# Two token pairs per turn in a 128-expert loop, expert counts formed on the matrix engine, and a shared final combination

## The chip, the cores and the metric

The kernel runs on one core of one Trainium2 chip. The metric is the device time of one launch in microseconds; three runs of the kernel before gave 1128.76, 1126.37 and 1127.86, so the median is 1127.86. In the text PE is TensorE, DVE is VectorE, ACT is ScalarE, POOL is GpSimd and SP is the engine that issues most transfers.

## The reference

Four sequences of 512 image tokens pass through softmax attention, get 77 text tokens appended (589 tokens, five tiles of 128 with the last partly empty), then a selective scan, a mixture of 14 experts, a causal attention, and last a mixture of 128 experts with two experts for each token. Layer normalization stands ahead of each of the last four. The change concerns the last two stages.

```python
scores = jnp.einsum('nqd,nkd->nqk', Q, K) / scale      # causal mask, softmax, times V
...
logits = xt @ wg                                       # 256 -> 128 experts
e1 = jnp.argmax(gates, -1); e2 = argmax of the rest
loc1 = (cumsum(mask1)[e1]) - 1                         # place of the token within its expert
loc2 = (cumsum(mask2)[e2] + counts1[e2]) - 1
buf  = rows placed at e*64 + loc (dropped from place 64 on)
yb   = jnp.einsum('ecd,edf->ecf', buf.reshape(128, 64, 256), we)
y    = (g1*v1) * yb[idx1] + (g2*v2) * yb[idx2]
h    = h + y
```

## The kernel before, in words

Every engine has one program, written out by hand in its order, and they meet only at semaphores. The token rows `Hs` are 20 tiles of 128 rows by 256 (`NB` = 4 sequences, `NT` = 5 tiles each).

**Causal stage.** For each sequence b, `project(b)` forms Q, K and V and `attend(b)` goes through five query tiles i: scores, mask and row maximum (`maxima`, DVE), exponential (ACT), transposes of the probabilities (L1267), their copy `PT4` (DVE, L2360), product with V (L1286), and the update of `Hs` (L2378). The routing of sequence b-1 to experts is woven in: normalized rows `xa5` (`rows5`), their turn (`turn_row`, L1160), copy `xaT5` (`turned5`, L1636), `logits` (L1166), `take_logits` (L2235) and `best_two`. For b of 2 and 3 the places of sequence b-2 are woven in too: `hots` makes the one-hot table `hot5` (L2253), `rank` on PE (L1181 to L1191) gives cumulative counts in three parts, `first_rows` on DVE (L2266) picks the places and writes the scatter indices `to5`, `second_rows` those of the second choice, and `count` (L2302, L2307) sums the table into `hsum`, which the next sequence's `rank` adds.

**Routing left over.** `two_experts` does the same for sequences 2 and 3 once attention is over. POOL scatters the rows with one indirect transfer per tile and choice (L1794), five and five for each sequence, and starts a sequence only when the five of the sequence before have landed.

**128-expert loop.** The experts go in 64 pairs; 128 gathered rows hold 64 rows for each of two experts. Four pairs are a group (16 groups). SP loads a group's rows `xg5` (four buffers) and 2 MB of weights (`ring`, six places). For pair j, PE turns the rows (`turn(j+1)` stands before `multiply(j)`): two 128x128 transposes against the identity on the full array, then one ACT copy to `xgT5` (L1716), then eight matmuls that each use half of the array's columns (L1343), then a DVE copy to `yo5` (L2445) and an indirect store by POOL (L1814).

**Combination.** SP loads `yg5` by sequence (four transfers); DVE does two multiply-adds per tile (L2452, 40 in all); SP stores each sequence when its ten are done.

The causal order of the places for sequence b-2 in the program of DVE before:

```python
if i == 0 and b >= 2:
    best_two(NT * (b - 1) - 1)
    hots(b - 2)
...
if b >= 2 and i in CHOICE_ROW:        # i = 1, 2, 3, behind the update of Hs
    first_rows(b - 2, CHOICE_BANK, part)
    if part == 2: second_rows(b - 2)
if b >= 2 and i == QT: count(b - 2)
```

Of the kernel before, what the change touches and what calls it, by code (L numbers as in the profile page):

```python
# [6 lines left out]
def fusion_kernel(nc, A, out):  # L7
# [22 lines left out]
    NP2 = NE2 // 2  # L30
    RING, LOAD = 32, 8
# [17 lines left out]
    with ctx:  # L49
# [147 lines left out]
        tri5 = tb("tri5", [P, 2, P], BF16)  # L197
# [11 lines left out]
        ejunk = tb("ejunk", [P, NT, NE2])  # L209
        hot5 = tb("hot5", [P, G, 2, NE2], BF16)  # L210
        hred = tb("hred", [P, 2, NE2])
# [34 lines left out]
        xgT5 = tb("xgT5", [P, 2, KC, P])  # L246
# [17 lines left out]
        act_acol = sem("act_acol")  # L264
# [114 lines left out]
        dve_hsum = sem("dve_hsum")  # L379
# [113 lines left out]
        CHOICE_BANK = (3, 7, 2)  # L493
        CHOICE_ROW = (1, 2, 3)
# [19 lines left out]
        def _(q):  # L514
# [138 lines left out]
            for g in range(NGR):  # L653
                if g + XG < NGR:
                    q.wait_ge(pe_xg5, GP * (g + 1))
# [12 lines left out]
            for b in range(NB):  # L668
                q.wait_ge(dve_h5, 2 * NT * (b + 1))
# [6 lines left out]
        def _(pe):  # L676
# [492 lines left out]
            def rank(b, banks, part):  # L1169
                pe.wait_ge(dve_hot5, b + 1)  # L1170
                if b:
                    pe.wait_ge(dve_hsum, b)
# [13 lines left out]
                if part == 2:  # L1186
# [3 lines left out]
                    if b:  # L1190
                        m = nc.tensor.matmul(taken, tri5[:, 1, :], hsum[:, (b - 1) % 2, 0, :], start=False, stop=True)  # L1191
                m.then_inc(pe_rank5, 1)

            def causal():
# [35 lines left out]
                def attend(b):  # L1230
# [24 lines left out]
                    scores(1)  # L1255
                    project_values(V_REST)
                    for i in range(NT):
# [11 lines left out]
                        m.then_inc(pe_pt4, 1)  # L1269
                        if i + 2 < NT:  # L1270
                            scores(i + 2)
                        elif i == NT - 1 and not last:
                            if b >= 2:
                                pe.wait_ge(dve_rank5, 3 * (b - 1))
                            turned(b + 1)
# [7 lines left out]
                        if i == 3 and b >= 2:  # L1283
                            pe.wait_ge(dve_rank5, 3 * (b - 2) + 2)
# [6 lines left out]
                        if b >= 2 and i in CHOICE_ROW:  # L1291
                            if i == 2:
                                pe.wait_ge(dve_h4, NT * b + 2)
                            part = CHOICE_ROW.index(i)
                            rank(b - 2, CHOICE_BANK, part)
# [8 lines left out]
            def two_experts():  # L1304
# [4 lines left out]
                for i in range(NT):  # L1309
# [5 lines left out]
                    if 1 <= i <= 3:  # L1315
                        rank(b - 1, (1, 5, 7), i - 1)
                logits(G - 1, homes[NT - 1])
# [6 lines left out]
                def turn(j):  # L1324
                    g, m = j // GP, j % GP
                    if m == 0:
                        pe.wait_ge(tile_in[g % XG], tile5_loads(g % XG, g // XG + 1))
                    if j >= 2:
                        pe.wait_ge(act_xg5, j - 1)
                    for c in range(KC):  # L1330
                        t = nc.tensor.transpose(ps[:, j % 2, P * c:P * (c + 1)], xg5[:, g % XG, m, P * c:P * (c + 1)], ident[:, :])  # L1331
                    t.then_inc(pe_xg5, 1)

                def multiply(j):
# [3 lines left out]
                    pe.wait_ge(act_xg5, j + 1)  # L1338
                    if j >= 4:
                        pe.wait_ge(dve_y5, j - 3)  # L1340
                    for c in range(KC):
                        for k in range(2):
                            t = nc.tensor.matmul(ps[CAP * k:CAP * (k + 1), 2 + j % 4, 0:D], xgT5[:, j % 2, c, CAP * k:CAP * (k + 1)],  # L1343
                                                 weights_of(g % PLACES)[:, 2 * m + k, c, :], start=(c == 0), stop=(c == KC - 1))
# [21 lines left out]
        def _(act):  # L1366
# [278 lines left out]

            def causal():
# [16 lines left out]
                def attend(b):  # L1663
                    last = b == NB - 1
                    for i in range(NT):
                        act.wait_ge(dve_nm4, NT * b + i + 1)
                        if i >= 2:
# [4 lines left out]
                                             accum_out=rs4[:, i:i + 1]).then_inc(act_p4, 1)  # L1672
                        if not last:
# [4 lines left out]
                        if b and i >= 2:  # L1678
                            turned5(NT * (b - 1) + i - 2, 5)
                        if b >= 2 and i == 2:  # L1680
# [5 lines left out]
                    if b:  # L1686
                        turned5(NT * b - 1, 3)
                entry_deviations(0)
# [10 lines left out]
            def two_experts():  # L1699
# [3 lines left out]
                for i in range(NT):  # L1703
                    if i + 1 < NT:
                        rows5(NT * b + i + 1)
                    turned5(NT * b + i, homes[i])
                sums5(b - 1)
# [4 lines left out]
                for j in range(NP2):  # L1712
                    act.wait_ge(pe_xg5, j + 1)
                    if j >= 2:
                        act.wait_ge(pe_y5, j - 1)
                    nc.scalar.activation(xgT5[:, j % 2, :, :], ps[:, j % 2, 0:D].rearrange("p (c t) -> p c t", c=KC), ACT.Copy).then_inc(act_xg5, 1)  # L1716
# [7 lines left out]
            nc.scalar.activation(acol[:, :], alog[:, :], ACT.Exp).then_inc(act_acol, 1)  # L1724
# [94 lines left out]
        def _(dve):  # L1819
# [340 lines left out]
            def one_expert():  # L2160
# [7 lines left out]
                dve.wait_ge(act_ex, 1)  # L2168
# [89 lines left out]
            def first_rows(b, banks, part):  # L2258
# [3 lines left out]
                dve.wait_ge(pe_rank5, 3 * b + part + 1)  # L2262
# [35 lines left out]

            def count(b):
                tiles = slice(NT * b, NT * (b + 1))  # L2300
                dve.wait_ge(dve_hot5, b + 1)
                link5(nc.vector.tensor_reduce(hred[:, :, :].rearrange("p k e -> p (k e)"),  # L2302
                                              hot5[:, tiles, :, :].rearrange("p m k e -> p (k e) m"), AX.X, ALU.add))
                if b:
                    dve.wait_ge(pe_rank5, 3 * b)
                    dve.wait_ge(dve_hsum, b)
# [261 lines left out]
```

## Time and profile before

| | us |
|---|---|
| median of the runs | 1127.86 |
| profiled execution | 1133.31 |
| its span | 1131.5 |
| PE busy, share of the span | 903.7, 80% |
| DVE busy | 742.5, 66% |
| ACT busy | 468.0, 41% |
| POOL busy | 206.8, 18% |
| mean granted clock of PE | 0.886 |

The profiled execution is one launch; 1.8 us of it lie outside the span. Times in all rows are microseconds from the start of the span. A row of the timeline is one instruction, or several of one kind merged (xN); its bracket is how long the engine was idle before it and what ended that. The granted clock is a share of 2.4 GHz, so 0.50 is 1.2 GHz. The end of a matmul is modelled.

### The profile page before, as it was taken

The page shows a single profiled execution, that of the slowest core. Times are in us where ns is not written, and L with a number is a line of the kernel's source. Part 1 is how long each engine was busy: PE and PEld are TensorE (multiplying, and loading weights), DVE is VectorE, ACT ScalarE, POOL GpSimd, SP SyncE. Part 2 cuts the span into 40 slices and gives each one's busy share as a digit, 9 for nine tenths or more (in the row PEclk, how much of TensorE's full clock was granted, in tenths as well). Part 3 has the DMA queues.
Part 4 walks back from the last instruction along what each step waited for, and adds up shares of the span by engine and source line. Part 5 has one row for each costly group of instructions (what it writes and reads, how often), then busy time and mean ns, then how long its engine had stood idle before and what let it go on. Part 6 is the DMA issues. An engine that isn't in the chain of part 4 may idle for free.

```text
span 1131.5 us, 14851 instructions
## 1 busy us (share of the span) xinstructions
PE 903.7 (80%) x4814; PEld 506.7 (45%) x4815; DVE 742.5 (66%) x1333; ACT 468.0 (41%) x903; POOL 206.8 (18%) x248
## 2 busy tenths in 40 slices
PE   7999979889898898975798289994999796278870
PEld 2323432344323443234565289994567665134430
DVE  4903689998999989999998401113567787712225
ACT  1175249760187602965786133443232431112210
POOL 1000001110011100111000613332000212646550
PEclk9999988896889968895899589998899998689995
DMA  3099526875068740797761366665205002079907
GB/s 108 2 323 270 171 87 170 216 173 148 1 172 214 175 129 0 191 224 175 234 204 83 124 185 196 206 188 204 100 1 205 35 11 89 10 272 400 395 28 273
DMA packets 75406, 180.77 MB, mean 160 GB/s; under 512 B 12155, under 2 KB 48718, under 8 KB 72657
## 3 DMA queue, kind: packets, MB, share of 16 engines
q1 hardware_dynamic: 60944, 143.28, 38.4%
q0 software_dynamic: 14400, 36.71, 14.9%
q8 instruction: 35, 0.57, 0.2%
q14 instruction: 27, 0.21, 0.1%
HBM read 120.05 MB, written 43.69 MB: 145 GB/s over the span
## 4 chain that ended last, share of the span: by engine, by line
PE 36%; DVE 29%; issue 19%; DMA 7%; POOL 5%; ACT 3%; SPq 1%; POOLq 0%; another core or an unknown queue 0%; DVEq 0%; ACTq 0%
DVE hst L1878 10%; PE ps L754 6%; PE ps L1343 5%; DVE mxn L1825 5%; DMA bc<-bc_dram 4%; PE ps L1213 3%; PE ps L1331 2%; PE ps L707 2%; POOL ys_dram L1783 2%; DVE hC L1886 2%; PE ps L1286 2%; PE ps L851 2%; DVE dBu L1867 2%; PE ps L1226 1%; DVE Hs L2452 1%
## 5 line engine op out<-in xcount | busy, mean ns | idle before, releaser
L1825 DVE TENSOR_REDUCE mxn<-ps 128x2 f32<-128x1024 f32 x128 | 150.0, 1219 | 65.9 <-PE ps L754 65.8
L1878 DVE TENSOR_TENSOR_SCAN hst<-dA,dBu 128x1180 f32<-128x1180 f32 x64 | 167.0, 2609 | 3.8 <-PE ps L882 3.2
L1424 ACT ACTIVATE Ph<-ps 128x1024 f32<-128x1024 f32 x128 | 125.1, 1074 | 29.1 <-PE ps L851 25.5
L754 PE MATMUL ps<-Kh,Qh 32*128 32x512 f32 x512 | 115.5, 731 | 11.9 <-DVE mxn L1825 9.3
L851 PE MATMUL ps<-Qh,Kh 32*128 32x512 f32 x512 | 117.3, 719 | 3.9 <-ACT Ph L1424 3.6
L1867 DVE TENSOR_TENSOR dBu<-dtu,bc 128x1180 f32<-128x1180 f32 x64 | 88.2, 1383 | 6.2 <-DMA bc<-bc_dram 4.8
L1762 POOL DMA_DIRECT2D yS<-hC x24 | 20.8, 866 | 380.9 <-DVE hC L1886 380.9
L2181 DVE TENSOR_TENSOR yo<-ps,b2r 128x256 f32<-128x256 f32 x32 | 13.6, 425 | 107.2 <-PE ps L1136 107.2
L1343 PE MATMUL ps<-ring,xgT 128*64 128x256 f32 x512 | 70.0, 395 | 13.4 <-ACT xgT L1716 9.5
L865 PE MATMUL ps<-Ph,Vh 128*32 128x512 f32 x512 | 74.4, 655 | 5.1 <-ACT OT L1428 3.3
L2445 DVE COPY yo<-ps 128x256 f32<-128x256 f32 x64 | 26.7, 423 | 76.9 <-PE ps L1343 62.8
L1814 POOL DMA_INDIRECT ys_dram<-yo,dest x64 | 62.2, 973 | 50.8 <-DVE yo L2445 30.8
L851 PEld LDWEIGHTS ps<-Qh,Kh 32*128 32x128 f32 x512 | 34.7, 203 | 79.1 <-issue 40.1
L1794 POOL DMA_INDIRECT xs_dram<-xa,to x40 | 39.4, 986 | 161.4 <-DVE to L2280 141.2
L707 PE MATMUL ps<-xT,wqk 128*128 128x512 f32 x128 | 63.1, 626 | 6.0 <-DMA wqk<-in_wqk 6.0
L1415 ACT ACTIVATE dA<-delta,acol 128x590 f32<-128x590 f32 x64 | 52.3, 817 | 32.5 <-DVE hst L1878 27.0
L754 PEld LDWEIGHTS ps<-Kh,Qh 32*128 32x128 f32 x512 | 35.8, 208 | 66.3 <-DVE mxn L1825 39.4
L1126 PEld LDWEIGHTS ps<-xgT,W 128*128 128x128 f32 x512 | 63.7, 196 | 3.4 <-ACT xgT L1593 1.8
L1886 DVE TENSOR_TENSOR hC<-hst,bc 128x1180 f32<-128x1180 f32 x48 | 65.1, 1362 | 0.0
L1126 PE MATMUL ps<-xgT,W 128*128 128x128 f32 x512 | 64.3, 280 | 1.0 <-ACT xgT L1593 1.0
L1716 ACT ACTIVATE xgT<-ps 128x256 f32<-128x256 f32 x64 | 23.8, 383 | 89.5 <-PE ps L1331 80.9
L1136 PE MATMUL ps<-W,hidT 128*128 x256 | 60.4, 379 | 0.0
(270 smaller groups left out, 1493.2 us busy)
## 6 DMA issues: line engine op xcount, KB each, us to landing
ring<-in_we SPq DMA_DIRECT2D x16, 2048.0 KB
bc<-bc_dram SPq DMA_DIRECT2D x48, 590.0 KB, 4.7
W<-in_w SPq DMA_DIRECT2D x46, 512.0 KB, 6.4
yS<-hC POOLq DMA_DIRECT2D x24, 590.0 KB, 6.8
yodd<-hC POOLq DMA_DIRECT2D x24, 590.0 KB, 6.8
xs_dram<-zeros SPq DMA_DIRECT2D x1, 8224.0 KB, 46.0
xg<-xs_dram SPq DMA_DIRECT2D x16, 514.0 KB
ys_dram<-zeros SPq DMA_DIRECT2D x1, 5120.0 KB, 50.6
```

The source lines that it names most:

```text
L707: m = nc.tensor.matmul(ps[:, bank, :], wqk[:, hg, which, c, :], xT[:, c, :], start=(c == 0), stop=(c == KC - 1))
L754: m = nc.tensor.matmul(ps[:, banks.start + hh % 2, :], Qh[HR * hh:HR * (hh + 1), hg, P * i:P * (i + 1)], Kh[HR * hh:HR * (hh + 1), hg, :], ...
L851: m = nc.tensor.matmul(ps[:, banks.start + hh % 2, :], Kh[HR * hh:HR * (hh + 1), hg, P * j:P * (j + 1)], Qh[HR * hh:HR * (hh + 1), hg, :], ...
L865: m = nc.tensor.matmul(ps[HR * hh:HR * (hh + 1), 4, :], Vh[:, j, 4 * hg + hh, :], Ph[:, n % 2, hh, :], start=(j == 0), stop=(j == QT - 1))
L1126: m = nc.tensor.matmul(ps[:, 2 + u, P * f:P * (f + 1)], W1[:, v, c, P * f:P * (f + 1)], xgT[:, u, c, :], start=(c == 0), stop=(c == KC - 1))
L1343: t = nc.tensor.matmul(ps[CAP * k:CAP * (k + 1), 2 + j % 4, 0:D], xgT5[:, j % 2, c, CAP * k:CAP * (k + 1)], weights_of(g % PLACES)[:, 2 * ...
L1424: nc.scalar.activation(Ph[:, n % 2, 2 * g:2 * g + 2, :], ps[:, turned_banks(b, 2 * n + g), :], ACT.Exp, scale=float(HD) ** -0.5).then_inc( ...
L1814: nc.gpsimd.indirect_dma_start(ys5_dram, bass.IndirectOffsetOnAxis(dest5[:, j:j + 1], 0), yo5[:, j // GP % YG, j % GP, :], None, bounds_ch ...
L1825: nc.vector.tensor_reduce(slots32(mxn[:, hg % 2, i, :])[:, 2 * g:2 * g + 2, HD], ps[:, score_banks(b, 2 * u + g), :], AX.X, ALU.max, negat ...
L1867: nc.vector.tensor_tensor(dBu[:, k % 2, :, :], dtu[:, :, :], bc[:, k % SLOTS, 0:1, :].to_broadcast([P, KC, LP]), ALU.mult).then_inc(dve_dB ...
L1878: nc.vector.tensor_tensor_scan(hst[:, k % 2, :, :].rearrange("p c t -> p (c t)"), dA[:, k % 2, :, :].rearrange("p c t -> p (c t)"), dBu[:, ...
L1886: nc.vector.tensor_tensor(gated(k), hst[:, k % 2, :, :], bc[:, k % SLOTS, 1:2, :].to_broadcast([P, KC, LP]), ALU.mult).then_inc(dve_hC, 1)
```

## The change

In the expert loop a step turns two pairs into one bank (`turn_two`), ACT copies 512 columns at once, and two multiplies follow. The counts `hsum` are formed by PE with an identity (`tally`) and copied by ACT (`tallied`), in place of DVE's `count`. In the causal stage `hots` moves from tile 0 to tile 1, the parts of `first_rows` go in front of the wait for the product with V in tiles 2, 3 and 4, `rank` moves accordingly, and `second_rows` goes behind. In the final combination tiles 3 and 4 of each sequence are formed by PE as diagonal(weights) times `yg5` and added by one DVE instruction; tiles 0 to 2 stay on DVE. The 32 diagonals are made by DVE in groups 3 to 6 of the expert loop. Semaphore `act_acol` is merged into `act_ex`, which changes no order.

```diff
 # DVE, attend(b)
                         if i == 0 and b >= 2:
                             best_two(NT * (b - 1) - 1)
+                        if i == 1 and b >= 2:
                             hots(b - 2)
+                        if i == 2 and b >= 2:
+                            first_rows(b - 2, CHOICE_BANK, 0)
                         if i + 2 < NT:
                             maxima(b, i + 2)
                         if b and i:
                             take_logits(...)
+                        if i >= 3 and b >= 2:
+                            first_rows(b - 2, CHOICE_BANK, i - 2)
...
-                        if b >= 2 and i in CHOICE_ROW:
-                            ... first_rows, second_rows
-                        if b >= 2 and i == QT:
-                            count(b - 2)
-                        if i and b:
+                        if b == 2 and i == QT:
+                            second_rows(b - 2)
+                        if i and b and not (b == NB - 1 and i == QT):
                             best_two(NT * (b - 1) + i - 1)
 # DVE, two_experts
                 variances(b)
+                second_rows(b - 2)
+                scales5(b)
+                best_two(NT * b - 2)
                 take_logits(NT * b - 1, 3)
                 best_two(NT * b - 1)
-                scales5(b)
                 hots(b - 1)
-                count(b - 1)
 # PE
+            def tally(b, bank):
+                pe.wait_ge(dve_hot5, b + 1)
+                dst = ps[:, bank, 0:D]
+                for t in range(NT):
+                    m = nc.tensor.matmul(dst, tri5[:, 2, :], hot5[:, NT * b + t, :, :] ...)
+                if b:
+                    m = nc.tensor.matmul(dst, tri5[:, 2, :], hsum[:, (b - 1) % 2, :, :] ...)
...
+                        if i == QT and b >= 2:
+                            pe.wait_ge(dve_h4, NT * b + QT)
+                            rank(b - 2, CHOICE_BANK, 2)
...
+                        if b >= 2 and i == 1:
+                            rank(b - 2, CHOICE_BANK, 0)
+                        if b >= 2 and i == 2:
+                            pe.wait_ge(act_p4, NT * b + QT)
+                            rank(b - 2, CHOICE_BANK, 1)
+                        if b >= 2 and i == QT:
+                            pe.wait_ge(dve_rank5, 3 * (b - 1))
+                            tally(b - 2, TALLY_BANK)
...
+                def turn_two(h):
+                    ...
+                    if h >= 2:
+                        pe.wait_ge(act_xg5, h - 1)
+                    for k in range(2):
+                        for c in range(KC):
+                            at = D * k + P * c
+                            t = nc.tensor.transpose(ps[:, h % 2, at:at + P], xg5[:, g % XG, m + k, P * c:P * (c + 1)], ident[:, :])
...
-                turn(0)
-                for j in range(NP2):
-                    if j + 1 < NP2:
-                        turn(j + 1)
-                    multiply(j)
+                turn_two(0)
+                for h in range(NP2 // 2):
+                    if h + 1 < NP2 // 2:
+                        turn_two(h + 1)
+                    multiply(2 * h)
+                    multiply(2 * h + 1)
+                for b in range(NB):
+                    pe.wait_ge(yg_in[b], 16 + 16)
+                    if b >= 2:
+                        pe.wait_ge(dve_h5, FIN * (b - 1))
+                    for i in range(FT, NT):
+                        for k in range(2):
+                            t = nc.tensor.matmul(ps[:, 6 + b % 2, at:at + D], diag5[:, b, i - FT, k, :], yg5[:, b, k, i, :], ...)
 # ACT, attend(b): turned5 in front of the next sequence's rows, sums5 one tile later
+                        if b and i >= 2:
+                            turned5(NT * (b - 1) + i - 2, 5)
                         if not last:
                             rows(b + 1, i)
...
+                for h in range(NP2 // 2):
+                    act.wait_ge(pe_xg5, h + 1)
+                    if h >= 2:
+                        act.wait_ge(pe_y5, 2 * h - 2)
+                    nc.scalar.activation(xgT5[:, h % 2, ...], ps[:, h % 2, :], ACT.Copy)
 # DVE, expert loop and combination
+                def diagonals(b):
+                    for i in range(FT, NT):
+                        for k in range(2):
+                            d = nc.vector.tensor_scalar(diag5[:, b, i - FT, k, :], ident[:, :], w5[:, NT * b + i, k:k + 1], None, ALU.mult)
+                    if DIAG_AT <= g < DIAG_AT + NB:
+                        diagonals(g - DIAG_AT)
+                    dve.wait_ge(pe_y5, NP2 + b + 1)
+                    nc.vector.tensor_tensor(rest, rest, ps[:, 6 + b % 2, 0:D * (NT - FT)], ALU.add)
```

## Rows read from the trace of the kernel before

**Rows 1.** The page: PE's busy time, share of the span, instructions.

```profile
PE 903.7 (80%) x4814; PEld 506.7 (45%) x4815; DVE 742.5 (66%) x1333; ACT 468.0 (41%) x903; POOL 206.8 (18%) x248
```

**Rows 2.** Busy time by stretch: length, busy us (instructions) by engine, PE clock, DMA share, GB/s.

```profile
865.00:907.00 42.00, 35.94 (x185) 26.14 (x184) 30.47 (x132) 13.72 (x42) 8.31 (x9) 1.00 0.36 151
907.00:945.00 38.00, 31.08 (x167) 23.05 (x166) 29.60 (x122) 9.12 (x31) 7.25 (x8) 1.00 0.03 8
...
996.00:1094.00 98.00, 85.34 (x602) 42.38 (x602) 25.23 (x73) 22.23 (x60) 55.89 (x58) 0.98 0.83 309
```

**Rows 3.** PE's waits, 865 to 907 (three rows), then 907 to 947: total, times, longest.

```profile
PE ps L1166 <- ACT xaT L1636: 2.6, 1, 2.6
PE ps L1286 <- DVE PT L2360: 2.4, 2, 1.7
PE ps L1201 <- DVE add L2284: 1.1, 1, 1.1
...
PE ps L1286 <- DVE PT L2360: 4.9, 2, 3.1
PE ps L1166 <- ACT xaT L1636: 2.1, 1, 2.1
```

**Rows 4.** Groups by line and shape, from 655 us on: busy, mean ns, idle before.

```profile
L1183 PE MATMUL ps<-hot,tri 128*128 128x256 bf16 x40 | 8.6, 322 | 0.0
L2302 DVE TENSOR_REDUCE hred<-hot 128x256 f32<-128x1280 bf16 x3 | 7.0, 2341 | 0.0
L2253 DVE TENSOR_TENSOR hot<-iota,bm 128x1280 bf16<-128x1280 f32 x4 | 6.0, 1492 | 0.1
L2307 DVE TENSOR_TENSOR hsum<-hsum,hred 128x256 bf16<-128x256 bf16 x2 | 0.9, 426 | 0.1
```

**Rows 5.** Timeline of POOL's scatters: first of sequence 2, first of sequence 3.

```profile
963.68 0.97 POOL L1794 DMA_INDIRECT xs_dram<-xa,to  x1 [13.69 <-DVE to L2280]
...
978.63 0.97 POOL L1794 DMA_INDIRECT xs_dram<-xa,to  x1 [2.16 <-issue]
```

**Rows 6.** Timeline of PE in the expert loop, one regular pair.

```profile
1011.08 0.44 PE L1331 MATMUL ps<-ident,xg 128*128 128x128 f32 x2
1011.45 1.08 PE L1343 MATMUL ps<-ring,xgT 128*64 128x256 f32 x8
1012.46 0.44 PE L1331 MATMUL ps<-ident,xg 128*128 128x128 f32 x2
```

**Rows 7.** Timeline of PE: first turns of the loop, and its last two multiplies.

```profile
996.69 1.11 PE L1331 MATMUL ps<-ident,xg 128*128 128x128 f32 x4 [21.02 <-DMA xg<-xs_dram]
...
1098.97 1.95 PE L1343 MATMUL ps<-ring,xgT 128*64 128x256 f32 x16
```

**Rows 8.** The group of the multiplies, and one late ACT copy in the timeline.

```profile
L1343 PE MATMUL ps<-ring,xgT 128*64 128x256 f32 x512 | 70.0, 395 | 13.4 <-ACT xgT L1716 9.5 <-issue 3.6
...
1027.87 0.66 ACT L1716 ACTIVATE xgT<-ps 128x256 f32<-128x256 f32 x2 [3.27 <-PE ps L1331]
```

**Rows 9.** Timeline: a POOL store, SP's last weight load; then two stretches as in rows 2.

```profile
1014.42 0.97 POOL L1814 DMA_INDIRECT ys_dram<-yo,dest  x1 [0.30 <-issue]
1061.11 0.34 SPq L636 DMA_DIRECT2D ring<-in_we  x1
...
1065.00:1075.00 10.00, 7.67 (x58) 3.69 (x55) 2.52 (x7) 2.19 (x6) 5.38 (x6) 1.00 1.02 379
1075.00:1085.00 10.00, 8.56 (x62) 4.33 (x64) 2.60 (x8) 2.19 (x6) 5.84 (x6) 1.00 0.19 57
```

**Rows 10.** The last store, the combination, a stretch in it, a DVE group of 512 columns.

```profile
1103.41 0.97 POOL L1814 DMA_INDIRECT ys_dram<-yo,dest  x1 [0.30 <-issue]
1111.71 15.92 DVE L2452 SCALAR_TENSOR_TENSOR Hs<-yg,w,Hs 128x256 f32<-128x256 f32 x40 [10.32 <-DMA yg<-ys_dram]
...
1114.00:1116.00 2.00, 0.00 (x0) 0.00 (x0) 2.00 (x6) 0.00 (x0) 0.00 (x0) 0.50 1.00 425
...
L2317 DVE TENSOR_SCALAR QK<-ps,bqk 128x512 f32<-128x512 f32 x16 | 12.0, 748 | 18.3 <-PE ps L1213 18.2
```

More of the change, by code:

```diff
@@ L1255, in attend @@
                     scores(1)
+                    if last:
+                        pe.wait_ge(act_hsum, b - 2)
                     project_values(V_REST)
@@ L1316, in two_experts @@
                         rank(b - 1, (1, 5, 7), i - 1)
+                    if i == 3:
+                        pe.wait_ge(dve_lg5, NT * b)
+                        tally(b - 1, 3)
                 logits(G - 1, homes[NT - 1])
@@ L1644, in sums5, with tallied @@
                                          accum_out=den[:, t:t + 1]).then_inc(act_den5, 1)
+            def tallied(b, bank):
+                act.wait_ge(pe_rank5, 4 * b + 4)
+                nc.scalar.activation(hsum[:, b % 2, :, :].rearrange("p k e -> p (k e)"), ps[:, bank, 0:D], ACT.Copy).then_inc(act_hsum, 1)
             def causal():
@@ L1677, in attend @@
                                 rows5(NT * (b - 1) + t)
-                        if b and i >= 2:
-                            turned5(NT * (b - 1) + i - 2, 5)
-                        if b >= 2 and i == 2:
+                        if b >= 2 and i == 3:
                             sums5(b - 2)
@@ L1710, in two_experts @@
                 nc.scalar.activation(w5[:, :, :], w5[:, :, :], ACT.Exp).then_inc(act_ex, 1)
[L1712 to L1716, printed above, removed]
+                for h in range(NP2 // 2):
+                    act.wait_ge(pe_xg5, h + 1)
+                    if h >= 2:
+                        act.wait_ge(pe_y5, 2 * h - 2)
+                    nc.scalar.activation(xgT5[:, h % 2, :, :, :].rearrange("p k c t -> p (k c t)"), ps[:, h % 2, :], ACT.Copy).then_inc(act_xg5, 1)
             act.preload_act_table_set("natural_log_exp_and_others")
@@ L2261, in first_rows @@
                 span = slice(NT * b + own.start, NT * b + own.stop)
[L2262 removed]
+                dve.wait_ge(pe_rank5, 4 * b + part + 1)
                 dve.wait_ge(dve_hot5, b + 1)
@@ L2297, in second_rows @@
                                                op0=ALU.add, op1=ALU.add).then_inc(dve_to5, 1)
[L2299 to L2306, printed above, removed]
-                    nc.vector.tensor_tensor(hsum[:, b % 2, :, :], hsum[:, (b - 1) % 2, :, :], hred[:, :, :], ALU.add).then_inc(dve_hsum, 1)
-                else:
-                    nc.vector.tensor_copy(hsum[:, 0, :, :], hred[:, :, :]).then_inc(dve_hsum, 1)
             def causal():
@@ L2448, in two_experts @@
                     for k in range(2):
-                        for t in range(NT * b, NT * (b + 1)):
+                        for t in range(NT * b, NT * b + FT):
                             if k:
-                                dve.wait_ge(dve_h5, 2 * NT * b + t - NT * b + 1)
+                                dve.wait_ge(dve_h5, FIN * b + t - NT * b + 1)
                             nc.vector.scalar_tensor_tensor(out=Hs[:, t, :], in0=yg5[:, b, k, t - NT * b, :], scalar=w5[:, t, k:k + 1],
                                                            in1=Hs[:, t, :], op0=ALU.mult, op1=ALU.add).then_inc(dve_h5, 1)
+                    dve.wait_ge(pe_y5, NP2 + b + 1)
+                    rest = Hs[:, NT * b + FT:NT * (b + 1), :].rearrange("p i d -> p (i d)")
+                    nc.vector.tensor_tensor(rest, rest, ps[:, 6 + b % 2, 0:D * (NT - FT)], ALU.add).then_inc(dve_h5, 1)
             dve.wait_ge(pool_init, 6)
```

75 lines of the change are left out of this document (40 added, 35 removed).

## The prediction

> **What bounds the kernel now.** I read the page first: PE is busy 80% of the span [rows 1], but the share mixes stages, so I went by stages with the windows view. Between 865 and 945 us (causal attention of sequences 2 and 3) PE works 67.0 of 80 us at full clock [rows 2]; the waits view says what the rest is: 13.1 us in which PE stood, all of it for DVE or for ACT behind DVE [rows 3]. From 996 to 1094 us (expert loop) PE works 85.3 of 98 us [rows 2] and its steady step is 1.38 us for a pair, from one turn to the next [rows 6]. The third view is the timeline around these places, and the last the chain of waits at the end: scatters of POOL up to 990 us, first multiply at 997.9, last store issued at 1103.41, then the load of `yg5`, the DVE multiply-adds from 1111.71 to 1127.63 and the last store [rows 10]. These stages come one behind another with nothing beside them, so gains in them add up. What comes before 830 us is not touched.
>
> **Causal stage and routing.** All prices are of the profiled execution (1133.31 us; the median of the runs is 5.45 lower).
>
> `hots` is 1.49 us of table [rows 4] plus four small ones, some 1.8 us together, and stands ahead of the maximum of tile 2, so probabilities, row copies and the ACT copy `xaT` are late and PE waits 2.6 and 2.1 us [rows 3]. In tile 1 it stands ahead of the maximum of tile 3, which PE needs only after scores, logits and two products with V, about 5 us on. It is not free: in tile 1 it also delays `take_logits`, for which the next turned row's bank waits. DVE needs 0.4 + 1.8 + 1.2 + 0.3 = 3.7 us from the copy of PT to the logits; PE has some 3.1 us to do meanwhile. I put 0.8 us of new wait there. `first_rows` of parts 1 and 2 today stand ahead of the copy of PT for tiles 3 and 4, hence the waits of 2.4 + 1.1 and 4.9 us [rows 3]; they now stand where DVE waits for the product with V (1.9 us in tile 3, 2.3 in tile 4), which covers the 1.3 and about 2.2 us that they take. Queued behind them is only the update of `Hs`, late by a few tenths. Part 0 goes ahead of the maximum of tile 4, and a new wait stands on PE before `rank` part 1 for the exponential of tile 3, which is done by then. Of 13.1 us I take 9 as gone (bounds: 4, if half of it reappears one tile later; 13.1, if nothing does). `tally` costs PE five or six matmuls of 256 columns, 0.11 us apart, 0.65 us twice: the row [rows 4] shows 0.32 us for one alone, so between 0.6 and 1.9 us each; I take 1.3 us in all because the ranks already run in series. Net 7.7.
>
> At the end of sequence 3 `count` runs with PE idle: 2.34 + 0.43 = 2.8 us [rows 4] go. The `count` of sequence 2 in `two_experts` (2.8 too) lies beside PE's row turns and is worth nothing to little. There `scales5`, which releases the last rows, gets `second_rows` (0.8 us) ahead of it and loses `take_logits` and `best_two` (0.9): even. `hots` behind it is later by about 1.4 us, which delays the first rank on PE by some 0.5: minus 0.5. For sequence 1 `turned5` ahead of a 0.59 us row gives back most of 1.1 us of PE's waits: I count nothing, as the room around it is unsure. Sum 7.7 + 2.8 - 0.5 = 10.0 us earlier for the first scatter of sequence 2 [rows 5]. From there POOL is the clock: ten scatters, 2.16 us of landing, ten more [rows 5], and DVE's places for sequence 3 are ready 4 to 5 us before POOL wants them, so the whole 10 us reach the loop. The five scatters of sequence 1 that `second_rows` now releases late take 6.4 us and have landed about 2 us before sequence 2 wants to start; if not, the difference is lost. Bounds 4 to 13.
>
> **Expert loop.** A regular pair is 0.37 us for the turn (1011.08 to 1011.45) and 1.01 for the multiply (to 1012.46) [rows 6]. Sixteen multiplies in a row, the last two pairs, take 1.95 us where eight take 1.08 [rows 6, 7], so a second multiply costs 0.87, not 1.01. Four transposes in a row at half clock take 1.11 us, one more thus 0.21, or 0.11 at full clock [rows 7]; a second turn costs 0.22, not 0.37. Two pairs cost 0.59 + 1.87 = 2.46 instead of 2.77: 0.31 us for each of 32 steps, 9.9 us.
> The Trainium skill says why that can be (TensorEngine Tiling (Array Packing), section Key Properties): changing the tiling mode drains the engine, and the turn uses the full array, the multiply half of its columns. The trace agrees (0.14 and 0.15 us per change above).
>
> Second, PE waited 13.4 us ahead of multiplies, in about ten places [rows 8]: DVE and ACT both saw PE's signals some 2.3 us late (1027.87, ACT idle 3.27 where 1.0 is usual). What causes it the trace does not say. A copy today has about 0.8 us of room; with two pairs per step and a copy of about 0.66 us (two copies back to back, [rows 8]) it has about 1.6. So each such place costs 0.8 us less, about 8 in all.
>
> But two other clocks then end last. POOL's store takes 0.97 + 0.30 = 1.27 us a pair [rows 9], more than PE's 1.23: from the first store (1001.2, now some 0.9 later for the longer first step) 64 of them end at 1083.5. And the DMA engines are full until about 1076.5 us (share 1.02, then 0.19; [rows 9]): the loop's last ten weight loads and twelve row loads, 27 MB, take from 1004 to there at some 400 GB/s, in one queue, and the order in it puts the rows of groups 14 and 15 behind the last weights. So PE gets group 14 not before 1075, has eight pairs left (9.8 us), and the last store ends at about 1087 against 1104.4: 17 us, 16 with one late signal in the last groups. The late signals earlier are hidden by this clock. The cover matters: without the DMA limit PE alone would end at 1079. Bounds 8 (a queue that runs 10% slower) to 20. The diagonals are 16 DVE operations of 128 columns, four per group; nearest rows 0.15 (a tiny one) to 0.42 (256 columns) each, 0.6 to 1.7 us a group, in idle time of DVE of about 0.9 us a pair, four banks deep: nothing.
>
> A rule speaks against them: the Trainium skill (SBUF — State Buffer, the "DVE blocks DMA" trap) says that POOL cannot write descriptors while DVE runs a fast mode from SBUF to SBUF; by it the sum would lose up to the diagonals' duration. No run here shows it yet.
>
> **Combination.** Ten multiply-adds are 3.98 us per sequence [rows 10]. Now six (2.39) and one add over 512 columns, 0.75 by its nearest row [rows 10]: 3.1 us. PE's four matmuls at half clock, 0.43 us each, 1.8 us, lie beside the six. The `yg5` pieces are 1.31 MB and arrive every 3.1 us at 425 GB/s [rows 10], so both clocks give 3.1 and the last update is at 1124.1 instead of 1127.6. The stores queue behind the loads; that costs about 0.5. Gain 3 (bounds 0, if the engines' queue decides, to 3.5).
>
> **Sum.** 10 + 16 + 3 = 29 us: the profiled execution would be 1104.3. Against the median it depends on where the 5.45 us lie that the profiled execution is longer: if all of them are late signals of the kind now hidden, the runs gain 23.5 (1104.4), if none, 29 (1098.9). I take the middle, 1101.5.
>
> **Rivals.** (B) The queue decides the loop sooner: demand rises from 2.6 MB in 6.3 us to 2.6 MB in 4.9 us, above what it delivered. If rows wait behind weights from group 10 on, the loop gains 8 instead of 16: 1109.5. For: share 1.0 for 70 us. Against: its end at 1076.5 is 24 us before PE's end today. (C) The waits of the causal stage move a tile on instead of going: gain 2 instead of 10: 1109.5. For: DVE is busy 30 of 42 us there [rows 2]. B and C together: 1117.5. (D) Slower: PE, starved by the queue, falls from 2.4 to 1.2 GHz in the loop. A pair then costs 2.46 instead of 1.23; from 22 pairs on (26.4 / 1.2) the whole gain is gone, at 32 pairs the time is 1141. For: after 21 us of idling the first turns ran at half clock [rows 7]. Against: waits up to 3.1 us left the clock at 1.00 [rows 2, 3], and the waits expected here are 1 to 3 us. (E) The diagonals hold POOL up: 16 times 0.2 us, 3.2: 1104.7.
>
> **Chances.** Forecast 0.60 (its own range 1095 to 1108), B 0.17, C 0.12, B and C 0.04, E 0.04, D 0.03. The likeliest gives 1101.5; the range 1094 to 1114 leaves out D, B with C, and the edges of the others. A difference under 0.2% (2.3 us) cannot be told from none. Faster 0.96, the same 0.01, slower 0.03.
>
> **What would show it.** Steps of two pairs 2.46 us apart; no wait of PE for PT or `add` between 865 and 945; the first scatter of sequence 2 near 954; first multiply near 988; PE waiting for `xg` or ring in the last four groups only; POOL's stores 1.27 us apart; `Hs` updates over about 12.4 us. The last store ends some 88 us after the first multiply (106 today); under 83 or over 97 the step on the loop is wrong, as it is if the clock falls in the loop.

## The result and the profile after

| | before | after |
|---|---|---|
| median of the runs, us | 1128.31 (4 runs, 1126.37 to 1129.85) | 1111.99 (4 runs, 1107.36 to 1114.40) |
| ratio with its 95% interval | | 0.9851 [0.9816, 0.9887] |
| profiled execution, and its span | 1133.31, 1131.5 | 1107.36, 1105.5 |

The kernel gained 16.3 us, and in a later comparison 17.3 (1109.07 against 1126.34, 0.9851 [0.9823, 0.9878]). The forecast was a gain of 26.4. The profiled execution of before lay 5 us above the median of its runs, that of after 4.6 below, so the two traces differ by 26 us where the medians differ by 16. Most of what follows is about that difference.

I read each trace in five pieces between marks that both kernels have: the first causal projection (p0), POOL's first scatter of sequence 2 (s2), the first turn of the expert loop (t0), the load of `yg5` (from there to the end is the tail), and the end.

| us | ahead of p0 | p0 to s2 | s2 to t0 | loop | tail | span |
|---|---|---|---|---|---|---|
| before, the trace of the prediction | 795.1 | 168.6 | 33.0 | 109.0 | 25.8 | 1131.5 |
| before, a second trace (`before_again`) | 795.3 | 171.6 | 33.1 | 98.6 | 26.0 | 1124.6 |
| after | 796.4 | 155.8 | 33.0 | 96.8 | 23.5 | 1105.5 |
| after, a second trace (`after_again`) | 794.7 | 155.9 | 33.0 | 98.7 | 23.3 | 1105.5 |

The causal stage gave 12.8 us against the first trace and 15.8 against the second (a third trace with the causal stage of before, `loop_only` below, took 171.3), the tail 2.3 and 2.5, and the loop 12.2 or, against the second trace, nothing that stands out of its own spread of 2 us.

**Causal stage.** The windows of after, columns as in [rows 2], then the loop's:

```profile
865.00:907.00 42.00, 40.09 (x208) 29.02 (x207) 31.82 (x139) 14.54 (x44) 7.63 (x8) 1.00 0.37 156
...
1005.00:1025.00 20.00, 20.00 (x165) 12.04 (x166) 10.43 (x36) 5.01 (x9) 15.11 (x17) 1.00 1.03 396
...
1045.00:1060.00 15.00, 11.22 (x92) 6.68 (x92) 3.62 (x10) 2.99 (x5) 8.44 (x9) 1.00 1.03 397
...
1066.00:1080.00 14.00, 10.89 (x92) 6.46 (x90) 4.42 (x12) 2.32 (x4) 9.12 (x11) 1.00 0.06 13
```

In 865 to 907 us PE now works 40.1 of 42 us, 35.9 before [rows 2]. PE's waits from p0 to s2 (engine, line waited for: total, times, longest), first in the second trace of before, then in after; [rows 3] are two stretches of the same view:

```profile
PE ps L1286 <- DVE PT L2360: 10.7, 9, 3.1
PE ps L1166 <- ACT xaT L1636: 6.3, 5, 2.6
PE ps L1160 <- ACT xa L1629: 5.4, 1, 5.4
PE ps L1213 <- ACT xT L1661: 1.9, 1, 1.9
PE ps L1201 <- DVE add L2284: 1.1, 1, 1.1
```
```profile
PE ps L1306 <- DVE PT L2398: 4.6, 7, 1.8
PE ps L1166 <- DVE lgb L2285: 2.9, 3, 1.4
PE ps L1166 <- ACT xa L1671: 2.4, 1, 2.4
PE ps L1230 <- ACT xT L1707: 1.9, 1, 1.9
PE ps L1187 <- DVE hot L2303: 1.1, 1, 1.1
PE ps L1187 <- DVE Hs L2421: 0.4, 2, 0.2
```

25.4 us have become 13.3, which is 12.1 of the gain. The first trace of before has the same waits (25.8, its `xa` 5.8) and was 3.0 us shorter in this piece for another reason: in the second trace PE ran at a lower clock in three places where it ran at full or fuller clock in the first. The projection at p0 took 11.92 us for 10.77; behind the wait of 2.6 us for `xaT` some 1.7 us were lost, and behind the wait of 3.1 us for PT some 1.1, where ten matmuls took 3.39 us for 2.43. The two places behind waits, from the second trace:

```profile
886.72 1.21 PE L1166 MATMUL ps<-wg,xaT 128*128 128x128 f32 x4 [2.62 <-ACT xaT L1636]
...
946.90 3.39 PE L1286 MATMUL ps<-V,PT 128*128 128x256 f32 x10 [3.09 <-DVE PT L2360]
```

The mean granted clock of the whole piece is 0.94 there, 0.96 in the first trace and 0.98 in after. So a wait in this stage has a second price, in some executions, of some 2.8 us in all here, and the change removed the two waits that carried it. The 1.15 us at p0 are not of that kind: there the traces of the changed order differ too (10.4 to 11.8 us).

**Loop.** PE's timeline in one regular two-pair step of after [rows 6], and its waits from 985 to 1085 us:

```profile
1004.94 1.95 PE L1372 MATMUL ps<-ring,xgT 128*64 128x256 f32 x16
...
1007.41 1.95 PE L1372 MATMUL ps<-ring,xgT 128*64 128x256 f32 x16
...
1037.58 0.66 PE L1359 MATMUL ps<-ident,xg 128*128 128x128 f32 x4 [2.35 <-DMA xg<-xs_dram]
1044.53 0.65 PE L1359 MATMUL ps<-ident,xg 128*128 128x128 f32 x4 [1.95 <-DMA xg<-xs_dram]
1051.43 0.65 PE L1359 MATMUL ps<-ident,xg 128*128 128x128 f32 x4 [1.91 <-DMA xg<-xs_dram]
...
1065.24 0.66 PE L1359 MATMUL ps<-ident,xg 128*128 128x128 f32 x4 [1.94 <-DMA xg<-xs_dram]
...
1073.22 3.67 PE L1372 MATMUL ps<-ring,xgT 128*64 128x256 f32 x32
```
```profile
PE ps L1359 <- DMA xg<-xs_dram: 32.2, 7, 21.1
```

From multiply to multiply the step takes 1007.41 - 1004.94 = 2.47 us, as forecast (2.46). But PE stands 32.2 - 21.1 = 11.1 us beyond the first wait, ahead of six of the sixteen groups, 9 to 14 counted from 0. Two groups start 6.9 us apart (1044.53, 1051.43) where their four pairs cost 4.9. The wait at 1065.24 is the one for group 14, the last. SP's queue and the chain of waits say why:

```profile
1034.09 6.62 SPq L655 DMA_DIRECT2D xg<-xs_dram  x1
1040.76 6.39 SPq L642 DMA_DIRECT2D ring<-in_we  x1
```
```profile
1025.85 18.63 DMA xg<-xs_dram
...
1047.25 17.95 DMA xg<-xs_dram
```

These groups of rows land 18 us after their issue, and the issue of a load alone holds SP's queue for 6.4 to 6.6 us. Full DMA engines alone don't bring that about: the last weight load of before was issued in 0.34 us [rows 9], with the share at 1.01 from 1055 to 1065 us. What does was not tried. The DMA share is 1.03 at some 400 GB/s up to 1060, then 0.06 after 1066.

**Tail.** DVE's timeline from 1084 us to the end of after, which answers to L2452 in [rows 10]:

```profile
1088.17 2.46 DVE L2499 SCALAR_TENSOR_TENSOR Hs<-yg,w,Hs 128x256 f32<-128x256 f32 x6 [10.81 <-DMA yg<-ys_dram]
1092.07 0.69 DVE L2503 TENSOR_TENSOR Hs<-Hs,ps 128x512 f32<-128x512 f32 x1 [1.43 <-PE ps L1390]
1092.67 2.46 DVE L2499 SCALAR_TENSOR_TENSOR Hs<-yg,w,Hs 128x256 f32<-128x256 f32 x6
1095.05 0.68 DVE L2503 TENSOR_TENSOR Hs<-Hs,ps 128x512 f32<-128x512 f32 x1
...
1100.99 0.68 DVE L2503 TENSOR_TENSOR Hs<-Hs,ps 128x512 f32<-128x512 f32 x1
```

The updates go from 1088.17 to 1101.67: 13.5 us, 15.9 before.

### The profile page after: what moved, and what is told of

It is laid out like the page before. It is cut to its first block and busy times, and to the rows that moved or that the text cites. A ratio compares the mean times of both kernels' runs of the same rounds, so it can differ in the third digit from the quotient of the medians.

```text
span 1105.5 us, 14861 instructions
## 1 busy us (share of the span) xinstructions
PE 905.1 (82%) x4863; PEld 517.0 (47%) x4864; DVE 734.0 (66%) x1331; ACT 465.3 (42%) x874; POOL 206.7 (19%) x248
## 5 line engine op out<-in xcount | busy, mean ns | idle before, releaser
L1372 PE MATMUL ps<-ring,xgT 128*64 128x256 f32 x512 | 62.7, 388 | 0.0
L1766 ACT ACTIVATE xgT<-ps 128x512 f32<-128x512 f32 x32 | 19.1, 597 | 82.7 <-PE ps L1359 82.7
## 6 DMA issues: line engine op xcount, KB each, us to landing
ring<-in_we SPq DMA_DIRECT2D x16, 2048.0 KB, 15.9
xg<-xs_dram SPq DMA_DIRECT2D x16, 514.0 KB, 13.2
```

## The experiments

Behind each label stands the median of its runs in us, then its ratio to before in the same comparison with the 95% interval; loops and tails are read from one trace each.

Theory one, from the table: the gain is the causal stage and the tail, and the loop is bound by its transfers in both kernels, so the two-pair step is worth nothing here. Its rival: the loop gave 10 us or more, since the late signals are the kernel's own and the two-pair step hides them.

**The step alone, and all but the step.** `loop_only` is before with `turn_two`, the copy of 512 columns and nothing else. `no_loop` is after with the one-pair step:

```diff
-                turn_two(0)
-                for h in range(NP2 // 2): ...
+                turn(0)
+                for j in range(NP2):
+                    if j + 1 < NP2: turn(j + 1)
+                    multiply(j)
 # ACT: one copy of 256 columns a pair; SP: wait_ge(pe_xg5, GP * (g + 1))
```

> The kernel before with the two-pair step of the expert loop alone; everything else as before. Theory: the three parts of the change add up, and the loop's part is 14.5 us of the profiled execution (first turn to landing of the last store 94.5 us instead of 109). Then the time is 1113 to 1116, PE waits for xg from group 9 on (some 11 us in all), and no late signals at ACT or DVE stop PE. Rival 1: the late signals (10 of them before, 13.4 us of PE's waits) belong to how often PE changes its mode; then they are gone here too. Rival 2: they come and go by chance or with where the code lies; then some may be back, hidden by the slack of two pairs, with ACT idle over 3 us in places outside the xg waits.

> The changed kernel with the expert loop's step of one pair put back; causal stage, counts and combination as changed. Theory: it loses the loop's part alone: 14 us, 1124 to 1127, with a loop of 107 to 109 us from first turn to last landing, and late signals that stop PE in about ten places. Rival: if the late signals were of one execution of the kernel before and not of its loop, the loop takes 88.6 + 8 = 97 us and the time is only some 3 us above the changed kernel, 1114 to 1116.

Measured: `loop_only` 1123.99 (10 runs) against 1125.78, 0.9986 [0.9959, 1.0013]. `no_loop` 1107.34 (4 runs), 0.9845 [0.98, 0.9889], the same as after. The loops last 98.4 and 97.2 us. So the step alone changes nothing that these runs can tell from none (the interval leaves room for at most 4.6 us), and its absence costs nothing. PE's turns with the idle time before them, from the groups of lines of `loop_only` and then of `no_loop`:

```profile
L1333 PE MATMUL ps<-ident,xg 128*128 128x128 f32 x128 | 22.4, 303 | 30.7 <-DMA xg<-xs_dram 30.7
```
```profile
L1357 PE MATMUL ps<-ident,xg 128*128 128x128 f32 x128 | 28.5, 307 | 24.1 <-DMA xg<-xs_dram 24.1
```

What the step saves on PE (28.5 to 22.4 in the turns alone) comes back as a longer wait for rows (24.1 to 30.7).

**Before, profiled again.**

> The kernel before, unchanged, profiled once more. The question is whether the 13.4 us in which late signals stopped PE in its expert loop belong to the kernel. Theory now (after four runs): they belong to that one execution; the loop is bounded by the DMA queue and takes 97 to 99 us from the first turn to the load of yg5, as in the four variants whose loops took 96.8 to 98.5, so the execution is 8 to 12 us shorter than the 1133.3 of the first. Rival: they belong to this kernel's one-pair loop in its place in the code; then the loop takes 107 to 109 us again.

Measured: span 1124.6, loop 98.6 us. PE's groups and a DMA window show no wait for `xgT` at all, and the queue full:

```profile
L1343 PE MATMUL ps<-ring,xgT 128*64 128x256 f32 x512 | 70.9, 399 | 0.1
L1331 PE MATMUL ps<-ident,xg 128*128 128x128 f32 x128 | 28.8, 309 | 24.3 <-DMA xg<-xs_dram 24.3
```
```profile
1045.00:1060.00 15.00, 15.00 (x111) 7.46 (x110) 4.68 (x14) 4.23 (x11) 10.61 (x12) 1.00 1.04 403
```

The 13.4 us of idle time ahead of multiplies in [rows 8] belonged to one execution. Of fourteen traces in this study it is the only one that has them; what made the signals late in it stays open.

**Is it the transfers?** If they bind, a lighter queue must bring the step's 9.9 us back. `light_two` is after and `light_one` is `no_loop`, both with each weight load inside the loop cut to a quarter of its bytes (two of its eight experts). They leave out the weights of the other six, which are computed with those of an earlier group:

```diff
-                    weights_load(g + PLACES)
+                    k = g + PLACES
+                    q.dma_start(weights_of(k % PLACES)[:, 0:2], A["we"][:, LOAD * k:LOAD * k + 2])...
```

> The changed kernel with the ten weight loads inside the expert loop cut to a quarter of their bytes; the other weights of a place are stale, so the results of those experts are not the reference's. Theory: the DMA queue bounds the loop of the changed kernel; without it PE never waits for xg, two pairs take 2.46 us, POOL's stores 1.27 us each end last, and from the first turn to the load of yg5 it takes 86 to 88 us instead of 96.8. Rival: POOL or late signals bound it; then it stays above 93.

> The same cut of the weight loads, with the one-pair step of the loop put back (the rest as changed); results of the stale experts are not the reference's. Theory: with the DMA queue out of the way the step decides: 64 x 1.384 us plus start and last store, 93 to 94 us from the first turn to the load of yg5, so the two-pair step is worth 6 to 7 us there (PE alone 9.9, of which POOL's 1.27 us a pair takes back 3). Rival: the step is worth nothing even here; then both take the same within 1 us.

Measured, one execution each: loops of 88.4 and 94.6 us. The step is worth 6.2 us there, and PE waits for rows only once in both. The windows of `light_two` and `light_one`:

```profile
1005.00:1070.00 65.00, 65.00 (x532) 39.11 (x530) 26.83 (x82) 15.52 (x26) 49.45 (x52) 1.00 0.57 172
```
```profile
1005.00:1070.00 65.00, 65.00 (x472) 32.28 (x470) 24.18 (x76) 18.02 (x47) 45.66 (x48) 1.00 0.61 176
```

It is 6.2 and not 9.9 because the next clock is POOL's: in `light_two` the first of its 64 stores starts at 996.09 and the last at 1076.97, 80.9 / 63 = 1.28 us a pair, above PE's 1.23, and the last multiply ends at 1071.84, four stores ahead. So the full queue costs the changed kernel 96.8 - 88.4 = 8.4 us or more.

**Another place for the row loads.** `split_w` loads each group's weights in two halves, the first as soon as two of a group's four pairs are multiplied; `xg_actq` issues the rows of groups 4 to 15 from ACT's queue, past SP's weights:

```diff
 # split_w, SP
+                    for half in range(2):
+                        q.wait_ge(pe_y5, GP * g + GP // 2 * (half + 1))
+                        q.dma_start(<half of the group's weights>)...
 # xg_actq, ACT, behind the copy of step h = 2 * (g + 2)
+                        act.wait_ge(dve_dest5, g + 1)
+                        nc.scalar.dma_start(xg5[:, g % XG, :, :], <rows of group g + XG>)...
```

> The changed kernel, with each weight load in the loop issued in two halves, the first when the first two pairs of the place's group are done. Theory: the DMA engines run without a gap from the first of these loads to the last, so what counts is when they start: 2.5 us earlier here, so the last rows land 2 to 2.5 us earlier and the loop is 2 to 2.5 us shorter; the time is 1109 to 1110 against the changed kernel's 1112. Rival: more and smaller transfers cost as much as the earlier start gives; no change, or the queue is full anyway and SP blocks: 1111 to 1113.

> The changed kernel with the loads of xg for groups 4 to 15 issued from ACT's queue, two groups ahead, instead of from SP's behind the weights. Theory: PE's 11 us of waits for xg in the loop come from the order in SP's queue: an xg load stands behind one or two weight loads of 2 MB, 18 us from issue to landing. On their own queue they land in a few us, PE waits only for the last weights, if at all, and the last store is 4 to 6 us earlier: 1106 to 1108. Rival: the DMA engines as a whole are the limit, whatever the order; then the waits move from xg to ring and the time stays within 1 us, 1111 to 1113.

`split_w`: 1112.69 (6 runs), 0.9874 [0.9846, 0.9902], loop 96.8: the same as after. `xg_actq`: 1126.76 (10 runs, 1114.70 to 1134.39), 0.9993 [0.9959, 1.0027], so it lost the whole gain. Its trace is of one of the fastest runs (1117.49), with a loop of 108.0. PE's timeline in it at three of the waits:

```profile
1010.59 1.11 PE L1355 MATMUL ps<-ident,xg 128*128 128x128 f32 x4 [5.88 <-DMA xg<-xs_dram]
1011.63 3.68 PE L1368 MATMUL ps<-ring,xgT 128*64 128x256 f32 x16
...
1030.35 1.06 PE L1355 MATMUL ps<-ident,xg 128*128 128x128 f32 x4 [2.02 <-DMA xg<-xs_dram]
1031.34 3.18 PE L1368 MATMUL ps<-ring,xgT 128*64 128x256 f32 x16
...
1053.51 0.66 PE L1355 MATMUL ps<-ident,xg 128*128 128x128 f32 x4 [3.56 <-DMA xg<-xs_dram]
1054.10 3.48 PE L1368 MATMUL ps<-ring,xgT 128*64 128x256 f32 x16
```

After each of the three the step that followed ran at half clock. The edit changes two things, the queue and the moment of issue, and the trace says which made the rows late. The rows of group 4, issued by SP in after and by ACT in `xg_actq`, with the chain of waits there:

```profile
987.23 0.36 SPq L655 DMA_DIRECT2D xg<-xs_dram  x1
```
```profile
995.48 15.06 DMA xg<-xs_dram
```

The changed kernel issues them 2.0 us behind its first turn, `xg_actq` 10.9 us behind, with the copy of the first step of group 2, and PE wanted them at 1004.7. From issue to landing a load of rows took 4.1 to 15.1 us (median 13.5) on ACT's queue, 3.9 to 18.6 (median 13.2) on SP's. So the own queue didn't make a load slower; the rows were late because the edit issued them three steps (one and a half groups) later. What the queue is worth with the old moment of issue was not tried.

**The tail.** `old_tail` is after with all ten multiply-adds of a sequence on DVE, without diagonals:

```diff
-                    if DIAG_AT <= g < DIAG_AT + NB:
-                        diagonals(g - DIAG_AT)
-                        for t in range(NT * b, NT * b + FT):
+                        for t in range(NT * b, NT * (b + 1)):
-                    dve.wait_ge(pe_y5, NP2 + b + 1)
-                    nc.vector.tensor_tensor(rest, rest, ps[:, 6 + b % 2, 0:D * (NT - FT)], ALU.add)...
```

> The changed kernel with the final combination all on DVE as before and without the 32 diagonals in the loop. Theory: the shared combination gave 2.5 us (20.3 minus 17.8 us from the landing of the first yg piece to the end of the span), and the diagonals cost nothing, so this runs 2 to 3 us longer than the changed kernel, 1114 to 1115. Rival: the diagonals hold up POOL's stores; then the loop here is up to 3 us shorter and the time equals the changed kernel's.

Measured: 1111.20 (4 runs), 0.986 [0.9814, 0.9905]; the runs alone can't tell it from after. Its trace can: tail 25.9 us against 23.5, with the old row back:

```profile
1092.50 15.92 DVE L2486 SCALAR_TENSOR_TENSOR Hs<-yg,w,Hs 128x256 f32<-128x256 f32 x40 [10.76 <-DMA yg<-ys_dram]
```

Its loop, 97.8 us, is no shorter without the diagonals, though a loop that waits for its rows would hide a small cost of theirs.

**The causal parts.** `old_order` puts `hots` back into tile 0 and `first_rows` behind the update, though in tiles 2 to 4 and not in 1 to 3 as before; `no_tally` gives the counts back to DVE:

```diff
 # old_order, DVE, attend(b)
                         if i == 0 and b >= 2:
                             best_two(NT * (b - 1) - 1)
+                            hots(b - 2)
-                        if i >= 3 and b >= 2:          # ahead of the wait for the product with V
-                            first_rows(b - 2, CHOICE_BANK, i - 2)
+                        if i >= 2 and b >= 2:          # behind the update of Hs
+                            first_rows(b - 2, CHOICE_BANK, i - 2)
 # no_tally
-                            tally(b - 2, TALLY_BANK)   # PE; and tallied on ACT
+                            count(b - 2)               # DVE
```

> The changed kernel with the causal stage's order on DVE partly undone: hots back in tile 0, ahead of the maximum of tile 2, and the three parts of first_rows back behind the update of Hs (tiles 2, 3, 4); tally on PE stays. Theory: the waits come back where they were: PE for xaT in tile 1 some 2 us and for PT in tiles 3 and 4 some 1.5 to 3 us, for each of sequences 2 and 3, so that from the first projection to the first multiply it takes 6 to 9 us more than the 189 to 190 of the changed kernel: 1118 to 1121. Rival: DVE's work is lighter without count, so the order is worth little; less than 3 us more.

> The changed kernel with the counts on DVE again (count behind the update of Hs in tile 4 and behind hots after attention), tally and its copy gone; order as changed. Theory: 2.8 us of count stand ahead of the statistics at the end of sequence 3 and come back in full; at the end of sequence 2 they are hidden by the projection, and the one after attention delays the logits by under 1 us; PE is 0.7 us shorter per sequence. Net 2 to 3 us more: 1114 to 1115. Rival: it is hidden, and the time equals the changed kernel's.

`old_order`: 1116.23 (5 runs), 0.9906 [0.9875, 0.9937], against 1109.07 for after in the same comparison; p0 to s2 164.8 us, 7.6 to 9.0 longer than in the nine traces with the new order and `tally` (155.8 to 157.2). PE's waits in it, 864 to 961 us:

```profile
PE ps L1204 <- DVE add L2334: 4.4, 2, 2.2
PE ps L1306 <- DVE PT L2398: 3.9, 4, 1.5
PE ps L1172 <- ACT xaT L1678: 3.2, 2, 1.6
```

In the whole piece they are 20.0 us for 13.3, and PE's busy time is 146.4 us for 144.0. The order is thus the larger part of the gain, and by the mechanism forecast. `no_tally`: p0 to s2 160.0 us, 2.8 to 4.2 longer, with PE waiting 4.9 us for `xa` at the end of attention instead of 2.4; its median of 1110.35 against 1109.07 can't be told apart. The two add up to 10.4 to 13.2 of the 12.8 to 15.8 us. The remainder (`scales5`'s place, the rows and `turned5` on ACT) was not tried by itself.

**After and `no_loop` again, in one comparison.**

> The changed kernel once more, beside the one with the one-pair loop put back, on one chip. Theory now: the two-pair step is worth nothing in this kernel, since the DMA queue bounds the loop in either form; 1108 to 1112, and the same as the other within 2 us.

> The changed kernel with the one-pair loop, once more. Theory: same as the changed kernel within 2 us (loop 97 us in both profiles), so the 4.6 us by which it was shorter the first time were the early part of the kernel, which differs from one execution to the next by up to 10 us ahead of any line that was changed. Rival: the one-pair form is faster by 4 us again; then the two-pair form has a cost that the first profile does not show.

1109.07 (5 runs), 0.9851 [0.9823, 0.9878], and 1110.69 (6 runs), 0.9876 [0.9845, 0.9908]: no difference, in a second comparison either. No complete version tried here beats the changed kernel by more than can be measured.

## Why the prediction was right in sign and 10 us too good

**Causal stage and routing: right, with a price left out.** Forecast 10 us (bounds 4 to 13), measured 12.8 against the trace that the forecast was made from, and 15.8 against the other. By its terms: of the 13.1 us of [rows 3] 1.0 are left, and 2.8 of the new wait for `lgb` (1.4 twice, where 0.8 was put), so 9.3 went for 9. `count` at the end showed as a wait for `xa` that fell from 5.4 or 5.8 to 2.4: 3.0 to 3.4 for 2.8. The later `hots` cost 1.1 us of wait for `hot`, for 0.5. Sequence 1 and the last `xaT`, counted as nothing, gave about 1. That is 12.2 to 12.6 without the price of `tally`, which PE's busy time doesn't show (143.8 us before, 144.0 after from p0 to s2, at 0.96 and 0.98 of the clock). What the forecast had no term for is the clock behind the waits, 2.8 us in the second trace of before. First scatter of sequence 2: 952.19 (forecast 954). The 33.0 us from scatter to loop stayed (32.8 to 33.2 in all traces), so all of it reached the loop, as said. Rival C is out.

**Loop: the step that failed.** It was the gain of 16 us, and it failed twice. First, and this is by far the larger part, 13.4 us of waits in ten places of one execution were taken as the kernel's; 8 of them were booked as gain, though the medians of before (1125 to 1128) have no room for them and a second trace has none. The sentence in the prediction that the profiled execution lay 5.45 us over the median was the hint: an excess of that kind should have gone to the rows for which the trace names no cause, and wholly, not by halves. Second, the queue. I had read the DMA share of 1.02 up to 1076 us as a limit that begins to bind only in the last four groups. In before without late signals it binds already: the share is 1.04 at 1045 to 1060, and PE waits 3.2 us beyond the first wait. Of the step's 9.9 us at most 1.8 reached the loop (98.6 to 96.8), in the second trace of after none (98.7). The place of the waits is nearly rival B's (group 10, 9 measured); B's time (1109.5, from a loop gain of 8) came near the measured one for a different reason, since it still counted late signals. The last store ended 93.5 us after the first multiply (1080.67 less 987.13) for a forecast of 88: inside the bounds of 83 to 97 that were to show the step wrong, as these too were worked out from the long loop of 106. The trace of after splits these 5 us. The rows of group 14 came 78.1 us after the first multiply, 76.2 in the forecast (1075 less 998.8), so the rate of the queue was read nearly right. From there the multiplies took 11.7 us (1065.24 to 1076.89) and not 9.8: a turn stands one step ahead of its multiplies, so ten pairs were left and not eight. And the last store ended 3.8 us after the last multiply, for 2.2 (1087 less 1084.8); before it was 3.5.

**Tail: right.** 2.3 to 2.5 us for 3. The mis-sized term is PE's part. The four matmuls of a sequence, put at 0.43 us each, are eight instructions; the first eight took 3.76 us at a granted clock of 0.50, not 1.8, so DVE, done with its six after 2.46, waited 1.43. From the second sequence on nothing waits: 2.98 us each for 3.1 forecast.

**Reconciliation.** The profiled execution was forecast at 1104.3 and took 1107.36: near, as 12.8 + 12.2 + 2.3 less 1.3 ahead of p0 came near 10 + 16 + 3. That was luck: 10 of the loop's 12.2 were the misfortune of one execution of before. From its second trace the gain is 15.8 + 1.8 + 2.5, less 1.0 ahead of p0; the medians say 16 to 17. The middle between "all" and "none" for the 5.45 us was a choice without a row behind it, and cost 3 of the 10.

**Rival E and the rule behind it.** There are 16 diagonals, as the prediction says, not 32. Four of them beside POOL's stores in after, from the timeline:

```profile
1007.28 0.96 DVE L2479 TENSOR_SCALAR diag<-ident,w 128x128 f32<-128x128 f32 x4
```
```profile
1006.71 0.97 POOL L1864 DMA_INDIRECT ys_dram<-yo,dest  x1 [0.30 <-DVE yo L2490]
1007.98 0.97 POOL L1864 DMA_INDIRECT ys_dram<-yo,dest  x1 [0.31 <-issue]
```

The store issued in the midst of them takes 0.97 us as ever, and its distance of 1.27 us is that of [rows 9]. The Trainium skill (SBUF — State Buffer, the "DVE blocks DMA" trap) says that POOL can't write descriptors during DVE's two-port modes from SBUF to SBUF. Its effect isn't seen here; whether this operation runs in such a mode no trace of ours shows.

**Rival D** did not come in the first trace of after: waits of 1.9 to 2.35 us left the clock at 1.00. It was nearer than it looked. In the second trace of after, the same kernel, waits of 1.94 and 1.92 us were followed by half clock:

```profile
1050.10 0.66 PE L1359 MATMUL ps<-ident,xg 128*128 128x128 f32 x4 [1.94 <-DMA xg<-xs_dram]
1050.69 2.83 PE L1372 MATMUL ps<-ring,xgT 128*64 128x256 f32 x16
...
1063.90 0.66 PE L1359 MATMUL ps<-ident,xg 128*128 128x128 f32 x4 [1.92 <-DMA xg<-xs_dram]
1064.49 2.97 PE L1372 MATMUL ps<-ring,xgT 128*64 128x256 f32 x16
```

The same came behind a wait of 2.22 us in `loop_only`, 2.02 in `xg_actq`, 2.16 in `split_w` and 2.20 in `old_order` (multiplies 3.2 to 3.6 us for 1.95), then full clock again within two steps. A fall like these costs PE some 1.6 us, not the 1.23 us a pair for the rest of the loop that D assumed. The first of the two above cost the loop nothing, as the next wait for rows (1.9 us in the first trace) went in its place; the second, behind the last wait, is most of the 1.9 us by which that loop is longer (98.7 for 96.8).

## What to carry to other kernels

Before a wait is booked as gain, ask whether the median has room for it: a trace whose time lies above its runs holds something that is not the kernel's, and a second trace is the cheapest experiment. When a DMA share stands at 1.0 over a stage, put the stage's bytes over its rate first and the engines' steps behind it; here 6.4 us off PE's turns (28.8 to 22.4) came back as 6.4 us more of waiting for rows (24.3 to 30.7). Work woven into another engine's waits, in the right tile, was the large gain: nearly the same instructions in another order gave some 8 of 17 us.

## What the runs showed of the hardware that was not expected

- Late in the loop a load's issue itself held SP's queue for 6.4 to 6.6 us, and rows of 0.5 MB landed 18 us after issue. In before, with a DMA share of 1.01, an issue took 0.34 us.
- Rows issued from ACT's queue, and one and a half groups later, made the loop 11 us longer (108.0 for 96.8), with 36.0 us of waits for 32.2; a load took no longer to land there (median 13.5 us for 13.2).
- In the loop, over all traces, six waits of 1.92 to 2.22 us and the two of 3.56 and 5.88 were followed by half clock, while 26 waits of 1.87 to 2.35 us were followed by full clock. The causal wait of 3.1 us was followed by full clock in one trace of before and by a lower one in the other. The same program draws either.
- The stretch ahead of p0, the same code in all kernels, took 793.5 to 804.8 us in fourteen traces: a spread of 11 us with which every single span has to be read.
